# A written-out, pipelined feed-forward whose normalised rows are made on GpSimd

## Chip, cores and metric

One core of one Trainium2 chip runs the kernel. The metric is the device time of one execution in microseconds (us). TensorE does the matmuls, VectorE, ScalarE and GpSimd the rest, SyncE issues the transfers.

## What is computed

The input `x` is 8 batches of 512 rows of 256. Three blocks act on it, and two of them are followed by the same feed-forward:

```python
x = x + attn_a(layernorm(x))          # 16 heads of 16, segments of 64 rows
x = x + ffn(layernorm(x))
x = attn_b(layernorm(x))              # a recurrence over 512 steps
x = x + ffn(layernorm(x))

def _ternary_linear(x, w):            # ffn = gelu between two of these, 256 -> 1024 -> 256
    alpha = jnp.mean(jnp.abs(w))
    w_t = jnp.sign(w) * (jnp.abs(w) > 0.5 * alpha).astype(w.dtype)
    rms = jnp.sqrt(jnp.sum(x * x, axis=-1, keepdims=True)) / jnp.sqrt(d)
    return jnp.einsum('bsd,fd->bsf', x / (rms + EPS), w_t)
```

So the ternary weights need the mean of all absolute weights first, and each feed-forward output row is divided by a root of the sum of squares of its 1024 hidden values.

## The kernel before

All of `x` stays on chip as 32 tiles of 128 rows (tile `b * 4 + u` is part `u` of batch `b`). Each engine has its own instruction stream, in the order the program writes it; counted semaphores (`F[...]` for the feed-forward, `A[...]` for the attention) join the streams. There is no planner.

**Attention** works batch by batch in units `w` (16 per batch, written out). Beside it, VectorE runs a scan over the absolute weights (`scan_lanes`, L1157), four pieces of 512 per batch, for which ScalarE takes the absolute values (L784) and SyncE loads the pieces; so all 32 pieces end with the last batch. After the last batch, TensorE transposes the sums (L592), and VectorE makes the convolution taps (L1207 to L1213), the thresholds (L1216 to L1225) and both ternary weight matrices (L1230, L1232), one after the other.

**Feed-forward** (`ffn_pe`, `ffn_act`, `ffn_dve`; called with 0 and with 1) is a loop over the 8 batches. For one batch of four tiles: VectorE takes statistics (L310 to L317), ScalarE a root (L286), VectorE scales (L322 to L326) and makes the normalised rows `xn` (L330). TensorE transposes them (L223), ScalarE writes the high half (L267), VectorE the low half (L341) of `xh`, each fp16. Then eight parts `n`: up matmuls (L237), Gelu (L274), high half (L282) and square (L283) on ScalarE, low half (L344) and sum of squares (L353, L356) on VectorE, down matmuls (L248). At the end come the sums over partitions (L253), ScalarE's root of them (L288), two small VectorE instructions (L361, L363) and the four rows sums back into `x` (L368). The root is in another activation table than Gelu, so ScalarE loads a table twice per batch (L274, L286). Eleven matmuls per batch (L226, L258) compute nothing that is used. The parts have two buffers: the Gelu of part `n` waits for the low half of part `n - 2`, and TensorE's order is up `n`, down `n - 1`. The transposes of the next batch stand behind all of this one's parts. The first feed-forward also takes the statistics that the recurrence needs (L295 to L302).

**Recurrence**: 512 steps on VectorE with GpSimd, ScalarE and TensorE beside it. GpSimd has no part in the feed-forward; in attention it takes eight small roots (L1394, L1397).

## Time and profile before

| what | value |
|---|---|
| median of 3 runs | 2784.52 us (2775.18 to 2790.23) |
| the profiled execution's own time | 2776.15 us |
| its span | 2774.3 us |
| VectorE, TensorE, ScalarE, GpSimd busy | 81%, 72%, 58%, 31% |
| granted TensorE clock, mean | 0.789 of 2.4 GHz |

The profile is of one execution. Busy shares are averages over stages with different limits: the attention takes about 466 us, the first feed-forward about 200, the recurrence with what lies around it about 1880, the second feed-forward about 208.

### The profile page before, as it was taken

What the parts mean: (1) busy time and instruction counts of PE and PEld (TensorE: products, weight loads), DVE (VectorE), ACT (ScalarE), POOL (GpSimd) and SP (SyncE); (2) the same over time, 40 slices, a digit from 0 to 9 for tenths busy, and PEclk for the clock granted to TensorE, in tenths of its full rate; (3) what the DMA queues carried; (4) which work ended last, traced back from release to release, by engine and by line L of the source; (5) the groups of instructions that cost most, each with busy time, mean ns of one, the idle gap of its engine ahead of it and who ended that gap; (6) DMA issues with size and microseconds to landing.
All of it is one profiled execution on the core that took longest, in us unless ns stands there. A gap on an engine that the chain in (4) does not pass through costs nothing. (4 is left out here: it accounts for less than half of the span.)

```text
span 2774.3 us, 47870 instructions
## 1 busy us (share of the span) xinstructions
PE 2001.7 (72%) x12529; PEld 1603.4 (58%) x12529; DVE 2252.9 (81%) x5774; ACT 1617.8 (58%) x4760; POOL 855.1 (31%) x1490
## 2 busy tenths in 40 slices
PE   6888886776877777677777777777786673435777
PEld 3555554443777666677666766767676662323444
DVE  6887886777059999999999999999999999991666
ACT  4888885775455555555555555555555554443676
POOL 0000000000034544545445454444545445440000
PEclk8999997999987776777777777776676766555999
DMA  5010000000000000000000000000000000000000
GB/s 161 16 27 18 16 22 9 0 0 0 0 1 0 0 0 0 0 1 0 0 0 0 0 0 0 0 0 0 0 0 1 0 0 0 0 0 0 15 23 23
DMA packets 14188, 23.28 MB, mean 8 GB/s; under 512 B 1280, under 2 KB 12032, under 8 KB 13824
## 3 DMA queue, kind: packets, MB, share of 16 engines
q1 hardware_dynamic: 14080, 21.97, 2.7%
q8 instruction: 52, 0.85, 0.1%
q14 instruction: 56, 0.46, 0.1%
HBM read 12.27 MB, written 4.19 MB: 6 GB/s over the span
## 5 line engine op out<-in xcount | busy, mean ns | idle before, releaser
L1458 POOL TENSOR_TENSOR wu<-U,stg 128x256 f32<-128x256 f32 x512 | 318.6, 622 | 853.3 <-DVE U L1385 853.3
L621 PE MATMUL bank<-U,ident 128*128 128x128 f32 x2080 | 471.1, 398 | 122.5 <-ACT go L883 103.7
L621 PEld LDWEIGHTS bank<-U,ident 128*128 128x128 f32 x2080 | 435.1, 253 | 163.7 <-issue 74.0
L684 PE MATMUL bank<-stack,tm 128*128 128x64 f32 x1792 | 349.5, 384 | 213.2 <-ACT tm L820 213.2
L1020 ACT ACTIVATE xs<-U 128x256 f32<-128x256 f32 x512 | 213.4, 417 | 469.4 <-DVE U L1385 467.6
L684 PEld LDWEIGHTS bank<-stack,tm 128*128 128x128 f32 x1792 | 338.2, 294 | 233.6 <-issue 233.6
L1335 DVE TENSOR_REDUCE pn<-xs 128x32 f32<-128x512 f32 x512 | 351.2, 686 | 29.2
L1415 POOL TENSOR_TENSOR kv<-stg 128x256 f32<-128x256 f32 x513 | 318.8, 621 | 1.6
L607 PE MATMUL bank<-wcat,yT 128*128 x1024 | 299.5, 452 | 3.0 <-issue 3.0
L949 ACT ACTIVATE small<-pn 128x16 f32<-128x16 f32 x513 | 110.8, 216 | 305.4 <-DVE pn L1335 305.4
L607 PEld LDWEIGHTS bank<-wcat,yT 128*128 128x128 f32 x1024 | 245.9, 251 | 30.7 <-issue 18.2
L1325 DVE TENSOR_TENSOR xs<-U,bank 128x256 f32<-128x256 f32 x512 | 215.3, 421 | 31.8 <-DVE U L1385 5.5
L1339 DVE TENSOR_TENSOR bank<-pn,bank 128x256 f32<-128x256 f32 x512 | 219.4, 429 | 17.8
L1347 DVE TENSOR_TENSOR bank<-wu,bank 128x256 f32<-128x256 f32 x512 | 218.8, 427 | 15.9 <-POOL wu L1458 0.7
L1385 DVE TENSOR_TENSOR U<-bank,kv 128x256 f32<-128x256 f32 x512 | 217.0, 424 | 17.6
L742 ACT ACTIVATE prob<-bank,nmax 128x128 f32<-128x128 f32 x512 | 181.3, 374 | 39.5 <-DVE nmax L1108 38.7
L248 PE MATMUL bank<-wdn,hh 128*128 128x256 f16 x1024 | 132.4, 272 | 65.9 <-ACT hh L282 41.0
L1379 DVE TENSOR_TENSOR kv<-bank,kv 128x256 f32<-128x256 f32 x384 | 163.0, 425 | 13.8 <-DVE bank L1363 0.4
L1411 POOL TENSOR_TENSOR stg<-R 128x128 f32 (+1 forms) x65 | 29.9, 460 | 461.6 <-ACT stg L904 461.6
L344 DVE SCALAR_TENSOR_TENSOR hh<-h,hh 128x512 f16<-128x512 f32 x128 | 88.2, 689 | 92.5 <-ACT hh L282 92.3
L248 PEld LDWEIGHTS bank<-wdn,hh 128*128 128x128 f16 x1024 | 92.6, 97 | 121.9 <-ACT hh L282 56.6
L820 ACT ACTIVATE tm<-bank 64x448 f32<-64x448 f32 x256 | 137.2, 536 | 17.3 <-PE bank L607 13.4
(185 smaller groups left out, 3753.6 us busy)
## 6 DMA issues: line engine op xcount, KB each, us to landing
out_x<-x SPq DMA_DIRECT2D x8, 512.0 KB, 2.9
x<-in_x SPq DMA_DIRECT2D x1, 3584.0 KB, 16.7
Vs<-V SPq DMA_DIRECT2D x8, 384.0 KB, 4.7
Vs<-V SPq DMA_DIRECT2D x8, 288.0 KB, 3.3
lane<-in_lanes SPq DMA_DIRECT2D x8, 256.0 KB, 5.1
wcat<-in_wcat SPq DMA_DIRECT2D x1, 1792.0 KB, 13.9
wraw<-in_w_up SPq DMA_DIRECT2D x1, 1024.0 KB, 18.6
wraw<-in_w_down SPq DMA_DIRECT2D x1, 1024.0 KB, 11.4
```

The lines of the kernel that those rows point to most:

```text
L248: last = pe.matmul(bank[4 + u][:, 0:D], hh[:, e % 2, part, u * P:(u + 1) * P], wdn[:, e, :], start=(e == 0 and part == 0), stop=(e == NF - ...
L607: last = pe.matmul(bank[1 + g][:, e * PB * H:(e + 1) * PB * H], yT[:, (pc // 2) % 2, k, pc % 2, 4 * g + 2 * e:4 * g + 2 * e + 2, :].rearra ...
L621: last = pe.matmul(rsum.rearrange("p (t i) -> p t i", i=HD), ident[:, :], steps[:, :, :, j], start=(j == 0), stop=(j == HD - 1))
L684: last = pe.matmul(bank[3 + g][:, e * CH:(e + 1) * CH], tm[:, g * (PB // 2) + e, :, :].rearrange("p a c -> p (a c)"), stack[:, :], start=T ...
L1020: act.activation(xs[:, 1, :], U[:, half, j, :], ACT.Square).then_inc(S["sq"], 1)
L1325: dve.tensor_tensor(ij(xs[:, 0, :]), u, row(kkz[:, jj, 0, :]), ALU.mult).then_inc(S["x"], 1)
L1335: dve.tensor_reduce(pn[:, :, :].rearrange("p a i -> p (a i)"), xs[:, :, :].rearrange("p a (i j) -> p (a i) j", j=HD), AXX, ALU.add).then_i ...
L1339: dve.tensor_tensor(ij(zz), col(pn[:, 0, :]), row(kkz[:, jj, 1, :]), ALU.mult).then_inc(S["z"], 1)
L1347: dve.tensor_tensor(zz, wu[:, :], zz, ALU.subtract).then_inc(S["d"], 1)
L1385: dve.tensor_tensor(U[:, half, j, :], zz, new, ALU.add).then_inc(S["u"], 1)
L1415: pool.tensor_tensor(ij(kv0[:, j % 2, :]), col(stg[:, half, j, TK, :]), row(stg[:, half, j, TV, :]), ALU.mult).then_inc(S["k0"], 1)
L1458: pool.tensor_tensor(ij(wu[:, :]), ij(U[:, half if j else 1 - half, (j - 1) % STEPS, :]), col(stg[:, half, j, TW, :]), ALU.mult).then_inc( ...
```

## The change

Five things change, all in and around the feed-forward:

1. The loop over batches becomes a written-out run over 8 **groups** `q`. A group is one tile from each of four batches (`tile(q, u)`), not four tiles of one batch. The output transfers follow the groups.
2. The groups are pipelined. TensorE transposes group `q + 1` between the parts 4 and 6 of group `q`, ScalarE and VectorE split it in the parts 5 to 7 (`xh` has two copies), and the outputs of group `q - 1` are scaled and added in the parts 2 to 5 of group `q`. Two output accumulators share one bank of PSUM, so that two groups fit.
3. GpSimd takes both roots (a power of 0.5) and makes the rows `xn` of the next group. ScalarE's roots and their table loads go, and so do the eleven unused matmuls.
4. The scan gets five pieces per attention batch and is done in batch 6. Thresholds, ternary weights, taps and the rows of group 0 are made by VectorE inside the last attention batch (`last_batch`).
5. The first of the eight sums of squares is no longer copied: the second part adds both squares.

```diff
+        def tile(q, u):
+            return ((q % 2) * 4 + u) * NT + q % B // 2
+        def tiles(q):
+            return slice(tile(q, 0), tile(q, NT - 1) + 1, NT)
...
+            def rows_transposed(q, k):
+                pe.wait_ge(F["xn"], q * NT + NT)
+                if q >= 2:
+                    pe.wait_ge(F["sr"], q if q % B == 0 else q - 1)
+                    pe.wait_ge(F["lo"], (q - 1) * KD + k + 1)
+                for u in range(NT):
+                    last = pe.transpose(bank[k][:, u * P:(u + 1) * P], xn[:, u, k * P:(k + 1) * P], ident[:, :])
+                last.then_inc(F["xt"], 1)
...
+            def up(q, n):
+                t = q * NF + n
+                if n == 0:
+                    pe.wait_ge(F["hi"], q * KD + KD)
+                    pe.wait_ge(F["lo"], q * KD + KD)
+                if t >= 2:
+                    pe.wait_ge(F["g"], t - 1)
+                for part in range(2):
+                    for k in range(KD):
+                        last = pe.matmul(bank[2 + n % 2][:, :], wup[:, k, n * P:(n + 1) * P], xh[:, q % 2, part, k, :],
+                                         start=(part == 0 and k == 0), stop=(part == 1 and k == KD - 1))
+                last.then_inc(F["up"], 1)
...
+                if e == 0 and q >= 2:
+                    pe.wait_ge(F["x"], (q - 1) * NT)
...
-                pe.wait_ge(F["g"], b * NF + NF)
-                for _ in range(6):
-                    pe.matmul(bank[2][:, :], identh[:, :], wup[:, 0, 0:512], start=True, stop=True)
...
+            for k in range(KD):
+                rows_transposed(i * B, k)
+            for q in range(i * B, i * B + B):
+                for n in range(NF):
+                    up(q, n)
+                    if q > i * B or n > 0:
+                        down(q * NF + n - 1)
+                    if n == 1 and q > i * B:
+                        square_sums(q - 1)
+                    if n in (4, 5) and q < i * B + B - 1:
+                        rows_transposed(q + 1, n - 4)
+            down((i * B + B) * NF - 1)
+            square_sums(i * B + B - 1)
...
-                act.wait_ge(F["ve"], b * 2 + (2 * i + 4))
-                act.activation(sd[:, :, :], vv[:, :, :], ACT.Sqrt).then_inc(F["sd"], 1)
-                act.wait_ge(F["sm"], b + 1)
-                act.activation(ysc[:, 0, :], bank[0][:, 0:NT], ACT.Sqrt, scale=1.0 / FF).then_inc(F["sr"], 1)
...
+                    if n in (5, 6) and q < i * B + B - 1:
+                        split_high(q + 1, n - 5)
...
+            for q in range(q0, q9 + 1):
+                for n in range(NF):
+                    t = q * NF + n
+                    dve.wait_ge(F["hh"], t + 1)
+                    dve.scalar_tensor_tensor(hh[:, t % 2, 1, :], h[:, t % 2, :], HI_H, hh[:, t % 2, 0, :],
+                                             ALU.mult, ALU.subtract).then_inc(F["hl"], 1)
+                    if n >= 1:
+                        s = q * (NF - 1) + n - 1
+                        dve.wait_ge(F["sq"], t + 1)
+                        if n == 1:
+                            old = hsq[:, 1 - t % 2, :]
+                        else:
+                            old = ssq[:, (s - 1) % 3, :]
+                            dve.wait_ge(F["ss"], s)
+                        if n == 3:
+                            dve.wait_ge(F["sm"], q)
+                        dve.tensor_tensor(ssq[:, s % 3, :], old, hsq[:, t % 2, :], ALU.add).then_inc(F["ss"], 1)
+                    if q < q9:
+                        if n == 0:
+                            row_stats(dve, q + 1)
+                            row_moments(dve, q + 1)
+                        if n == 2:
+                            row_scales(dve, q + 1)
+                        if n in (6, 7):
+                            split_low(q + 1, n - 6)
+                    if q > q0:
+                        if n == 2:
+                            read_sums(q - 1)
+                        if n == 4:
+                            output_scales(q - 1)
+                        if n in (4, 5):
+                            add_rows(q - 1, (2 * n - 8, 2 * n - 7))
+                        if i == 0 and n in (6, 7):
+                            next_stats(q - 1, (2 * n - 12, 2 * n - 11))
+                        if i == 0 and n == 7:
+                            next_moments(q - 1)
...
+        def ffn_pool(pool, i, beside_first):
+            def row_roots(q):
+                pool.wait_ge(F["ve"], 2 * q + 2)
+                pool.tensor_tensor(sd[:, :, :], vv[:, :, :], halves[:, :, :], ALU.pow).then_inc(F["sd"], 1)
+            def output_roots(q):
+                pool.wait_ge(F["sr"], q + 1)
+                pool.tensor_tensor(ysc[:, 1, :], ysc[:, 0, :], halves[:, 0, :], ALU.pow).then_inc(F["s1"], 1)
+            q0, q9 = i * B, i * B + B - 1
+            def rows_normalised(q):
+                pool.wait_ge(F["sc"], q + 1)
+                pool.wait_ge(F["xt"], q * KD)
                 for u in range(NT):
...
+                    pool.tensor_scalar(xn[:, u, :], x[:, tile(q, u), :], mv[:, u, 0:1],
+                                       rstd[:, u:u + 1], ALU.subtract, ALU.mult).then_inc(F["xn"], 1)
+            row_roots(q0)
+            for q in range(q0, q9 + 1):
+                if q < q9:
+                    row_roots(q + 1)
+                    rows_normalised(q + 1)
+                if q > q0:
+                    output_roots(q - 1)
+            output_roots(q9)
...
-                    if (w - 5) % 3 == 0 and w < 17:
-                        c = (w - 5) // 3
-                        act.wait_ge(w_ld, b * 16 + 16)
-                        act.activation(lane[:, c * PIECE:(c + 1) * PIECE], lane[:, c * PIECE:(c + 1) * PIECE],
-                                       ACT.Abs).then_inc(w_abs, 1)
+                    if (w - 5) % 3 == 0 and b * PIECES + (w - 5) // 3 < 4 * B:
+                        c, piece = divmod(b * PIECES + (w - 5) // 3, 4)
+                        part = lane[:, piece * PIECE:(piece + 1) * PIECE]
+                        act.wait_ge(w_ld, c * 16 + 16)
+                        act.activation(part, part, ACT.Abs).then_inc(w_abs, 1)
...
+            def last_batch(w):
+                if w == 5:
+                    thresholds()
+                if w in (6, 7, 8, 9):
+                    ternary((w - 6) // 2, w % 2)
+                if w == 11:
+                    convolution_taps()
+                if w == 13:
+                    row_stats(dve, 0)
+                    row_moments(dve, 0)
+                if w == 15:
+                    row_scales(dve, 0)
+                    rows_normalised(dve, 0, range(NT))
...
+                    if b == B - 1 and w == 4:
+                        pe.wait_ge(w_car, B + 1)
+                        pe.wait_ge(A["rp"], B * 6 * NT)
+                        pe.transpose(bank[3][:, 0:2 * LANES], carry[:, 0:1].to_broadcast([2 * LANES, P]),
+                                     ident[0:2 * LANES, 0:2 * LANES]).then_inc(w_lan, 1)
```

How the streams move. **VectorE**, from part 7 of one batch to its outputs, before (`den`, `rstd` are the scales of the next batch, `ysc` those of the outputs):

```order
L344 SCALAR_TENSOR_TENSOR hh<-h,hh 128x512
L356 TENSOR_TENSOR ssq<-ssq,hsq 128x512
L321 REGISTER_ALU
L322 SCALAR_TENSOR_TENSOR den<-sd 128x4
L324 RECIPROCAL rstd<-den 128x4
L326 TENSOR_SCALAR rstd<-rstd 128x4
L328 REGISTER_ALU
L330 TENSOR_SCALAR xn<-x,mv,rstd 128x256 x4
L361 TENSOR_SCALAR ysc<-ysc 128x4
L363 RECIPROCAL ysc<-ysc 128x4
L368 ISA
L368 SCALAR_TENSOR_TENSOR x<-bank,ysc,x 128x256
```

VectorE now, from part 2 of a group to part 4 (L391 is the low half, L403 the sum of squares, L327 to L331 the scales of the next group, L347 the sums of the group before, L351 and L353 its output scales):

```order
L391 SCALAR_TENSOR_TENSOR hh<-h,hh 128x512
L403 TENSOR_TENSOR ssq<-ssq,hsq 128x512
L327 SCALAR_TENSOR_TENSOR den<-sd 128x4
L329 RECIPROCAL rstd<-den 128x4
L331 TENSOR_SCALAR rstd<-rstd 128x4
L347 TENSOR_SCALAR ysc<-bank 128x4
L391 SCALAR_TENSOR_TENSOR hh<-h,hh 128x512
L403 TENSOR_TENSOR ssq<-ssq,hsq 128x512
L391 SCALAR_TENSOR_TENSOR hh<-h,hh 128x512
L403 TENSOR_TENSOR ssq<-ssq,hsq 128x512
L351 TENSOR_SCALAR ysc<-ysc 128x4
L353 RECIPROCAL ysc<-ysc 128x4
```

The scales stand between parts, the four instructions for `xn` are gone from this engine, and the output scales stand two parts behind the scales.

**GpSimd**, from the attention into what follows, before:

```order
L1395 UNCONDITIONAL_BRANCH
L1395 ISA
L1397 TENSOR_TENSOR sd<-vv,halves 128x4
L1395 REGISTER_ALU
L1395 COMPARE_AND_BRANCH
L1411 TENSOR_TENSOR stg<-R 128x8x16
L1401 TENSOR_TENSOR wtmp<-wtmp,decay 128x128
```

GpSimd now, in the first feed-forward (L433 the root of the statistics, L444 the rows `xn`, L437 the root of the output sums; `ISA` is an instruction that sets the engine up):

```order
L433 TENSOR_TENSOR sd<-vv,halves 128x8 x2
L444 ISA
L444 TENSOR_SCALAR xn<-x,mv,rstd 128x256 x4
L433 TENSOR_TENSOR sd<-vv,halves 128x8
L444 TENSOR_SCALAR xn<-x,mv,rstd 128x256 x4
L437 TENSOR_TENSOR ysc<-ysc,halves 128x4
```

The four rows instructions stand ahead of the output root in GpSimd's order, and TensorE's transposes wait for all four.

**VectorE in the last attention batch**, now (L1193 maxima, L1200 a copy, L1223 and L1229, L1231 the outputs, L1266 and L1270 the ternary weights); before, none of L1266 and L1270 stood here, and a scan piece (L1157) stood in every third unit:

```order
L1193 TENSOR_REDUCE nmax<-bank 128x4
L1266 TENSOR_SCALAR wneg<-wraw,thr 128x2048
L1193 TENSOR_REDUCE nmax<-bank 128x4
L1200 COPY probT<-bank 128x512
L1270 SCALAR_TENSOR_TENSOR wup<-wraw,thr,wneg 128x2048
L1229 TENSOR_TENSOR x<-x,bank 128x256
L1231 TENSOR_TENSOR x<-x,bias_a 128x256
L1193 TENSOR_REDUCE nmax<-bank 128x4
L1214 RECIPROCAL rden<-den_a 128x16
L1216 COPY rdx<-rden 128x256
L1266 TENSOR_SCALAR wneg<-wraw,thr 128x2048
```

The long weight instructions now stand between the maxima of neighbouring units.

## Rows read from the trace of the kernel before

**Rows 1.** Busy time by stage, whole core: stretch, then busy us (instructions), PEclk, DMA.

```profile
330.00:385.00 55.00, 46.65 (x635) 29.61 (x632) 44.42 (x95) 47.60 (x181) 0.00 (x0) 1.00 0.08 19
...
424.00:466.00 42.00, 33.84 (x451) 21.78 (x449) 25.23 (x48) 28.45 (x121) 0.00 (x0) 0.83 0.01 2
...
466.00:486.00 20.00, 4.91 (x19) 2.99 (x20) 15.62 (x42) 2.80 (x5) 0.00 (x0) 0.53 0.00 0
...
2574.00:2772.00 198.00, 150.66 (x971) 90.95 (x969) 133.40 (x334) 139.78 (x237) 0.00 (x0) 1.00 0.06 19
```

**Rows 2.** Timeline from attention to the end of the first feed-forward: start us, us, engine.

```profile
465.51 0.42 DVE L1146 TENSOR_TENSOR x<-x,bias_a 128x256 f32<-128x256 f32 x1
...
478.80 0.21 ACT L262 ACTIVATE sd<-vv 128x8 f32<-128x8 f32 x1 [15.32 <-DVE vv L317]
...
479.66 1.38 DVE L330 TENSOR_SCALAR xn<-x,mv,rstd 128x256 f32<-128x256 f32 x4
...
481.10 1.97 PE L223 MATMUL bank<-ident,xn 128*128 128x128 f32 x8 [15.84 <-DVE xn L330]
...
485.89 0.60 ACT L274 ACTIVATE h<-bank 128x512 f32<-128x512 f32 x1 [0.89 <-PE bank L237]
...
683.75 0.17 DVE L302 COPY mean_b<-mv_b 128x8 f32<-128x8 f32 x1
```

**Rows 3.** Timeline of the second feed-forward, from one batch into the next.

```profile
2592.52 0.95 PE L253 MATMUL bank<-ones,ssq 128*128 128x1 f32 x8
...
2595.01 1.09 PE L223 MATMUL bank<-ident,xn 128*128 128x128 f32 x8 [0.22 <-DVE xn L330]
...
2595.78 1.09 ACT L267 ACTIVATE xh<-bank 128x512 f16<-128x512 f32 x2 [2.10 <-PE bank L223]
...
2597.00 1.28 DVE L341 TENSOR_TENSOR xh<-bank,xh 128x512 f16<-128x512 f32 x2
...
2598.52 1.90 PE L237 MATMUL bank<-xh,wup 128*128 128x512 f16 x8 [1.34 <-DVE xh L341]
...
2599.59 0.60 ACT L274 ACTIVATE h<-bank 128x512 f32<-128x512 f32 x1 [1.42 <-PE bank L237]
...
2600.22 0.63 ACT L282 ACTIVATE hh<-h 128x512 f16<-128x512 f32 x1
...
2600.88 0.69 DVE L344 SCALAR_TENSOR_TENSOR hh<-h,hh 128x512 f16<-128x512 f32 x1 [2.60 <-ACT hh L282]
...
2601.67 1.03 PE L248 MATMUL bank<-wdn,hh 128*128 128x256 f16 x8 [1.26 <-ACT hh L282]
```

**Rows 4.** Chain of waits in the same stretch: start us, us, what.

```profile
2601.67 1.03 PE bank L248 x8
...
2602.70 0.88 PE bank L237 x4
...
2605.73 1.03 PE bank L248 x8
...
2623.34 1.05 PE bank L237 x4
```

**Rows 5.** Groups of instructions by line: count, busy us, mean ns, idle before.

```profile
L324 DVE RECIPROCAL rstd<-den 128x4 f32<-128x4 f32 x18 | 3.2, 178 | 0.6
...
L1420 POOL TENSOR_SCALAR ge<-ge 128x256 f32<-128x256 f32 x64 | 54.6, 854 | 5.4
...
L1406 POOL TENSOR_SCALAR stg<-wtmp 128x128 f32<-128x128 f32 x65 | 42.0, 646 | 0.4 <-ACT wtmp L918 0.4
...
L1397 POOL TENSOR_TENSOR sd<-vv,halves 128x4 f32<-128x4 f32 x6 | 6.0, 1008 | 281.8 <-DVE vv L1063 281.8
...
L1157 DVE TENSOR_TENSOR_SCAN lane<-lane 32x512 f32<-32x512 f32 x24 | 30.4, 1265 | 0.0
```

**Rows 6.** Timeline inside the recurrence: VectorE and GpSimd at the same moment.

```profile
1500.25 0.42 DVE L1325 TENSOR_TENSOR xs<-U,bank 128x256 f32<-128x256 f32 x1
...
1500.30 0.62 POOL L1458 TENSOR_TENSOR wu<-U,stg 128x256 f32<-128x256 f32 x1 [1.14 <-DVE U L1385]
```

## Prediction before the run

> **What bounds the kernel now.** I read the windows by stage first, then the timelines of the two places that the change touches, then the chain of waits. The windows [rows 1] show what it can reach: the second feed-forward keeps TensorE busy for 151 of 198 us at a granted clock of 1.00 (the higher of its two levels, 2.4 GHz), ScalarE for 140, VectorE for 133. So no engine is full, and the stage goes by a chain. Rows 4 show that chain: two parts take 2605.73 - 2601.67 = 4.06 us, and one batch 24.82 (from the up matmuls at 2598.52 [rows 3] to those at 2623.34). The 4.06 are the loop through two buffers: the down matmuls and the up matmuls behind them 1.03 + 0.88 [rows 4], then Gelu to high half 0.63, to low half 0.66, to the next down matmuls 0.79 [rows 3], and some 0.07 of handing over between them. Eight parts so cost 16.3 us, and 8.5 of 24.8 lie between batches: table loads, roots, rows, transposes and splits, one after another [rows 3]. The other place is the way from attention to the first feed-forward [rows 2]: attention's last VectorE instruction ends at 465.93, and the first Gelu starts at 485.89. In these 20 us TensorE does 4.9 us of work at half the clock [rows 1].
>
> **One group of the new feed-forward.** It keeps the loop of the two buffers, so its floor is again 16.3 us. To it come, on TensorE or in front of it:
> - the sums of squares, 0.95, and the transposes, 1.09 [rows 3]; both now stand between parts.
> - a wait for `xn`. Count from the start of the low half of part 2. VectorE does that and the sum (0.6 each from start to start, as the two splits in rows 3 stand), then three scale instructions (0.18 [rows 5] and a little for waiting on one another): at 1.9, handing over included, GpSimd can begin. TensorE starts down 2 at 0.8 (0.69 and 0.1), up 4 at 1.7, down 3 at 2.7 (it needs the next low half) and is free for the transposes at 3.6. GpSimd's four rows instructions are not in the trace: nearest is its tensor_scalar of the same size at 0.854 us [rows 5]. Bounds are 0.62, its two-input instruction of that size [rows 6], and 1.01, its dearest [rows 5]. I take 0.85: `xn` is there at 1.9 + 3.4 + 0.1 = 5.4, TensorE waits 1.8.
> - the end of the group. The next up needs the second low half of `xh`, and VectorE makes that only behind part 7. Up 7 to its Gelu takes 1.03 and one more Copy of 0.55 ahead of it on ScalarE [rows 3], then 0.63, 0.66 to the low half, another 0.6 and 0.6 for it and the sum, 0.68 for the split, 0.1: 4.9 to 5.2, where a part takes 2.04. So 3.0 more.
> - less 0.9, since the parts beside these waits run shorter than 2.04, having been held back before.
>
> Sum 16.3 + 2.0 + 1.8 + 3.0 - 0.9 = **22.3 us**, against 24.8. The statistics of VectorE (behind part 0) and, in the first feed-forward, those for the recurrence lie beside the sums of squares and the end of the group. GpSimd's output root (1.01) stands behind `xn` and keeps VectorE waiting for about 1 us in part 4, with nothing due in that time: the low half of part 5 comes 2 us later, behind the transposes. Per 0.1 us that a rows instruction takes longer, the group takes 0.4 longer, both feed-forwards 5.6.
>
> **What GpSimd and VectorE do to each other** is the unknown. In the recurrence an instruction of VectorE with one operand in SBUF and one in PSUM takes 0.42 us beside a running one of GpSimd, and this pair stands there 512 times [rows 6]: nothing is lost. But low half and sum of squares read two tensors in SBUF, and none of that kind meets GpSimd anywhere in this trace. The lower end is nothing (22.3). The upper end is that each waits for the other's whole instruction. Then low halves and sums of parts 3 and 4 step in between the four, the root and `xn` wait for them and they for `xn`: about 3.1 us (three or four times 0.69, and 0.6 on the way back), 25.4 a group. Between: GpSimd's tensor_scalar takes 0.646 for 128 elements and 0.854 for 256 [rows 5], so 0.41 of 0.85 grows with the elements. If only this part collides, two of VectorE's instructions step in, 1.2 us: **23.5** a group. I take this, nearest to what rows 5 show of how such an instruction spends its time.
>
> The Trainium skill has a rule that speaks against the change: the page "SBUF — State Buffer", section "SBUF: two separate sides", says that a VectorE instruction with two SBUF inputs and a GpSimd instruction that reads SBUF exclude each other for the whole instruction. By it the upper end would hold. No row here can show it; it is rival B.
>
> **The sum**, against the profiled execution's own 2776.15 us:
> - Both feed-forwards, from the first group to the last: 7 x (24.82 - 23.5) = 9.2 each, -18.5. First and last group change ends that about cancel: the last roots cost 1.01 on GpSimd, a table load of 1.28 goes.
> - Way into the first feed-forward. The rows of group 0 are ready in the last attention batch, so TensorE transposes at 466.05 instead of 481.10 [rows 2]. Then as before: -14.6 after the splits. TensorE now has no unused matmuls to raise its clock: the eight transposes take 1.97 instead of 1.09 [rows 2, 3], and its first up matmuls are slow too: +1.5.
> - The last attention batch takes over what VectorE did from 465.93 to the end of the rows at 481.04 (taps, thresholds, weights, statistics, scales, rows; 15.1 us [rows 2]) and gives up four scan pieces of 1.27 [rows 5]: +10 on an engine that is idle for 17 of the last 42 us [rows 1], which is 1 us per unit, in the gaps between units. Between 0 and 10; half hidden, +5.
> - Six more scan pieces in batches 0 to 5, where VectorE is idle for 10.6 of 55 us [rows 1], and two fewer in batch 6: 4 x 1.27 = 5, half hidden: +2.5. SyncE's order of piece and shifted values keeps both a unit or two ahead: 0.
> - Into the second feed-forward: GpSimd's root 1.01 for ScalarE's 0.21 [rows 5, 2], +0.8, and the colder clock, +1.
> - Output transfers are as large as before and the last is again one: 0. Written-out code: 0.
>
> Sum -18.5 - 14.6 + 1.5 + 5 + 2.5 + 1.8 = **-22 us**, 2754 for such an execution. Its time lies 8 us below the median of the runs shown, so against 2784.5 I forecast **2762 us**.
>
> **Rivals.**
> - A, no collision: 22.3 a group, 7 x 1.2 x 2 = 17 less, 2745. For it: rows 6. Against: they have no instruction with two SBUF operands. 0.25.
> - B, whole instructions exclude each other: 25.4, 27 more than forecast, 2789. The feed-forward then loses 8 us, and only the way into it gains. 0.25.
> - C, slower: as B, and a rows instruction with its two per-partition scalars takes more than the tensor_scalar of rows 5, which has none. From 1.03 us on the kernel is over 0.5% slower (0.18 x 56 = 10 on top of B's 4); at 1.2 it takes 2808. Place: the transposes in part 4, which wait for all four. 0.12.
> - D, slower: the clock. The unused matmuls are gone; where the granted clock falls to its lower level, the blocks of matmuls of 0.88 us [rows 4] take twice as long. If that holds for a quarter of the 16 in a group, it is 3.5 us a group, 49 in all: 2811. Against: TensorE is busy for 16 of 23.5 us, not far from the 151 of 198 at 1.00 [rows 1], and waits longer than 2 us only at the transposes. 0.05.
> - Forecast: 0.33 and within 10 us of 2762 for the attention's half-hidden terms.
>
> **Numbers.** 0.5% is 14 us, about what a measurement here can tell from none. Faster by more holds A and three quarters of the forecast: 0.50. Within it are B and the rest of the forecast: 0.31. Slower: C, D and the edge of B, 0.19. The range runs from A with a gain in the last batch, 2738, to B with 10 us more, 2799.
>
> **What would show it.** In the profile after: distance of first up matmuls between groups 23.5 (22.3 in A, 25.4 in B); GpSimd's `xn` instructions at 0.85 and idle time of VectorE or stretched low halves beside them; idle time of TensorE before the transposes of part 4, released by GpSimd, 3 us; first Gelu near 480; last attention batch 5 us longer; granted clock 1.00 in both feed-forwards. A clock below 0.9 there, or first Gelu later than 486, would make the prediction wrong.

## The result, and the profile after

The change makes the kernel slower: 2822.3 us median of 4 runs (2803.7 to 2827.0) against 2783.4 (2775.2 to 2790.2) before, ratio 1.013 with a 95% interval of 1.007 to 1.018. Forecast were 2762 us and a range from 2738 to 2799. The profiled execution took 2826.6 us (span 2824.5), 50 more than that of before. By stage, between the same events of the two traces:

| stretch | before | after | difference |
|---|---|---|---|
| start to the end of attention's last add | 465.9 | 484.6 | +18.7 |
| from there to the first Gelu | 20.0 | 5.4 | -14.6 |
| first Gelu to the last add of feed-forward 1 | 195.9 | 220.9 | +25.0 |
| recurrence with both ways, to the next first Gelu | 1893.0 | 1896.4 | +3.4 |
| feed-forward 2 | 196.0 | 213.8 | +17.8 |

So the way into the first feed-forward paid what was forecast, and both feed-forwards, which should have become 9 us shorter each, became longer. The first Gelu starts at 490.1, 4 us later than before, because attention ends later; a start behind 486 was one of the prediction's signs of being wrong, and so was a clock below 0.9. The windows by stage show the clock (columns as in [rows 1]):

```profile
484.00:712.00 228.00, 161.02 (x896) 97.41 (x896) 135.06 (x366) 119.92 (x209) 66.75 (x43) 0.83 0.00 1
2622.00:2822.00 200.00, 141.18 (x833) 86.47 (x831) 110.76 (x265) 108.83 (x191) 61.40 (x38) 0.88 0.06 19
```

The granted clock, 1.00 in the second feed-forward before [rows 1], is 0.88 there and 0.83 in the first. The timeline of the way into the first feed-forward, which answers to [rows 2]:

```profile
484.20 0.42 DVE L1231 TENSOR_TENSOR x<-x,bias_a 128x256 f32<-128x256 f32 x1
...
484.73 1.94 PE L230 MATMUL bank<-ident,xn 128*128 128x128 f32 x8 [1.02 <-issue]
...
490.07 0.60 ACT L299 ACTIVATE h<-bank 128x512 f32<-128x512 f32 x1 [1.47 <-PE bank L242]
```

The transposes begin 0.1 us behind the last add, at the lower clock level (1.94 us for eight). The timeline of the second feed-forward, parts 3 and 4 of a group, answers to [rows 3] (start us, us, engine):

```profile
2642.76 6.88 POOL L444 TENSOR_SCALAR xn<-x,mv,rstd 128x256 f32<-128x256 f32 x4 [2.23 <-DVE rstd L331]
2642.77 0.71 DVE L391 SCALAR_TENSOR_TENSOR hh<-h,hh 128x512 f16<-128x512 f32 x1
2643.40 0.68 DVE L403 TENSOR_TENSOR ssq<-ssq,hsq 128x512 f32<-128x512 f32 x1
...
2643.62 1.03 PE L254 MATMUL bank<-wdn,hh 128*128 128x256 f16 x8
...
2644.93 0.69 DVE L391 SCALAR_TENSOR_TENSOR hh<-h,hh 128x512 f16<-128x512 f32 x1 [0.86 <-ACT hh L304]
...
2649.61 1.02 POOL L437 TENSOR_TENSOR ysc<-ysc,halves 128x4 f32<-128x4 f32 x1
...
2649.69 1.08 PE L230 MATMUL bank<-ident,xn 128*128 128x128 f32 x4 [5.04 <-POOL xn L444]
...
2650.57 1.91 PE L242 MATMUL bank<-xh,wup 128*128 128x512 f16 x4
2650.67 0.17 DVE L351 TENSOR_SCALAR ysc<-ysc 128x4 f32<-128x4 f32 x1 [4.44 <-POOL ysc L437]
...
2652.52 0.60 ACT L299 ACTIVATE h<-bank 128x512 f32<-128x512 f32 x1 [7.10 <-PE bank L242]
```

This is the place. GpSimd begins `xn` at 2642.76, 0.1 us behind the scales, and takes **6.88 us for four instructions**, where I had 3.4 without a collision and 4.6 with the one that I took. VectorE's low halves and sums go on beside it at 0.68 to 0.71. TensorE waits 5.04 us, ScalarE's next Gelu 7.10, and VectorE 4.44 for the output root, which stands behind `xn`. TensorE then works on at 1.91 instead of 1.03.

Eleven of the fourteen groups look like this. In the other three TensorE waits only 3.4 to 3.5 us, and in two of them VectorE is held up too. One of the two, in the first feed-forward:

```profile
583.45 5.70 POOL L444 TENSOR_SCALAR xn<-x,mv,rstd 128x256 f32<-128x256 f32 x4 [3.74 <-DVE rstd L331]
...
583.69 0.85 DVE L391 SCALAR_TENSOR_TENSOR hh<-h,hh 128x512 f16<-128x512 f32 x1
```

There the low half starts 0.24 us behind the first rows instruction and not 0.01. It takes 0.85 instead of 0.69, and the four rows instructions take 5.70 instead of 6.88.

The chain of waits of the second feed-forward (answers to [rows 4]) has it twice:

```profile
2642.76 6.89 POOL xn L444 x4
...
2649.69 1.08 PE bank L230 x4
2650.78 1.71 PE bank L242 x4
...
2658.26 2.27 issue
2660.53 1.86 PE bank L242 x4
```

Behind the wait a block of four up matmuls takes 1.71 where [rows 4] had 0.88. The same happens behind the 2.27 us between groups (2660.53). First up matmuls of neighbouring groups are 28.0 us apart here (2632.56 to 2660.53) and 27.4 from group to group on the average of this feed-forward, against 24.8. The groups by line (answers to [rows 5]: busy us, mean ns, idle before):

```profile
L444 POOL TENSOR_SCALAR xn<-x,mv,rstd 128x256 f32<-128x256 f32 x56 | 92.8, 1667 | 31.1 <-DVE rstd L331 31.1
...
L391 DVE SCALAR_TENSOR_TENSOR hh<-h,hh 128x512 f16<-128x512 f32 x128 | 88.9, 695 | 126.8 <-ACT hh L304 126.5
...
L433 POOL TENSOR_TENSOR sd<-vv,halves 128x8 f32<-128x8 f32 x16 | 30.4, 1900 | 427.3 <-DVE vv L323 427.3
```

VectorE's low halves have a mean of 695 ns, against 689 before, the two held up included. GpSimd's rows instruction has a mean of 1667 ns, and in the eleven groups the four take 2.25, 2.24, 1.22 and 1.22.

### The profile page after: what moved, and what is told of

Read it like the earlier page. It is cut to its first block and busy times, and to the rows that moved or that the text cites. A ratio compares the mean times of both kernels' runs of the same rounds, so it can differ in the third digit from the quotient of the medians.

```text
span 2824.5 us, 46550 instructions
## 1 busy us (share of the span) xinstructions
PE 2024.0 (72%) x12353; PEld 1613.5 (57%) x12353; DVE 2224.8 (79%) x5672; ACT 1568.7 (56%) x4695; POOL 992.4 (35%) x1578
## 5 line engine op out<-in xcount | busy, mean ns | idle before, releaser
L1445 DVE TENSOR_TENSOR bank<-pn,bank 128x256 f32<-128x256 f32 x512 | 219.5, 429 | 17.8
L391 DVE SCALAR_TENSOR_TENSOR hh<-h,hh 128x512 f16<-128x512 f32 x128 | 88.9, 695 | 126.8 <-ACT hh L304 126.5
L242 PE MATMUL bank<-xh,wup 128*128 128x512 f16 x512 | 158.5, 441 | 36.6 <-issue 33.7
L433 POOL TENSOR_TENSOR sd<-vv,halves 128x8 f32<-128x8 f32 x16 | 30.4, 1900 | 427.3 <-DVE vv L323 427.3
L299 ACT ACTIVATE h<-bank 128x512 f32<-128x512 f32 x128 | 76.3, 596 | 186.1 <-PE bank L242 185.4
L254 PE MATMUL bank<-wdn,hh 128*128 128x256 f16 x1024 | 147.3, 291 | 20.5 <-DVE hh L391 18.5
```

The lines of the kernel that those rows point to most:

```text
L1445: dve.tensor_tensor(ij(zz), col(pn[:, 0, :]), row(kkz[:, jj, 1, :]), ALU.mult).then_inc(S["z"], 1)
```

## The experiments

My theory after this reading: three things add up. The rows instruction takes 1.22 us by itself; VectorE holds it up; and TensorE's long wait costs a second time by the clock.

The kernels below were measured in three further rounds, each together with the kernel before, whose median was 2774.9, 2775.9 and 2780.7 us there and 2783.4 in the round of the change. So two medians from different rounds can be out against one another by some 8 us. Differences from the change are given by medians; by the ratios to the kernel before they are smaller for what gained: 64 us instead of 81 for e1, 21 instead of 32 for e3, 23 instead of 36 for e4.

### e1: the rows back on VectorE

```diff
                         if n == 2:
                             row_scales(dve, q + 1)
+                        if n == 2:
+                            rows_normalised(dve, q + 1, range(NT))
...
                     row_roots(q + 1)
-                    rows_normalised(q + 1)
```

> Edit: the four rows instructions go back to VectorE, behind the scales in part 2; GpSimd keeps both roots. Theory (GpSimd's rows instruction, 1.22 us alone and 2.24 beside a low half and a sum, makes TensorE wait 5.04 us per group, and the clock falls behind that wait): the wait before the transposes is gone (under 0.5 us), the granted clock in both feed-forwards is back at 0.95 or more, a group takes about 22 us instead of 27.7, so 14 x 5.7 = 80 us less than the change: about 2742, faster than the kernel before. Rival 1 (the clock falls because the eleven unused matmuls are gone, whatever the wait): clock stays near 0.85, group near 24, about 2770. Rival 2 (GpSimd's roots or the order of the outputs hold the group): group stays over 26, no less than 2800.

2741.5 us, ratio to before 0.990 (0.986 to 0.994), as expected. Which engine makes the rows decides, by itself, between slower and faster. The timeline of its second feed-forward:

```profile
2632.19 1.38 DVE L337 TENSOR_SCALAR xn<-x,mv,rstd 128x256 f32<-128x256 f32 x4
...
2633.72 3.19 POOL L439 TENSOR_TENSOR ysc<-ysc,halves 128x4 f32<-128x4 f32 x1 [3.39 <-DVE ysc L347]
...
2634.39 1.03 PE L254 MATMUL bank<-wdn,hh 128*128 128x256 f16 x8 [1.28 <-DVE hh L391]
...
2635.26 0.60 PE L230 MATMUL bank<-ident,xn 128*128 128x128 f32 x4
...
2644.37 1.02 PE L242 MATMUL bank<-xh,wup 128*128 128x512 f16 x4 [2.28 <-issue]
```

Four rows take VectorE 1.38 us, TensorE transposes without any wait, and this group takes 21.2 us (2623.19 to 2644.37); the average is 21.6 in the second and 22.5 in the first feed-forward. The granted clock is 0.96 in its second and 0.93 in its first feed-forward, with no unused matmul: rival 1 is out as the main cause, though the clock, which was 1.00 before, is still down behind the wait of 2.28 us between groups in some of them. The output root on GpSimd, 1.02 in the change, now takes 3.19 beside four of VectorE's long instructions; VectorE waits 0.90 for it.

### e3: VectorE's work beside the rows made small

```diff
+                    e = slice(0, 1 if n in (3, 4) else L)
-                    dve.scalar_tensor_tensor(hh[:, t % 2, 1, :], h[:, t % 2, :], HI_H, hh[:, t % 2, 0, :],
+                    dve.scalar_tensor_tensor(hh[:, t % 2, 1, e], h[:, t % 2, e], HI_H, hh[:, t % 2, 0, e],
...
-                        dve.tensor_tensor(ssq[:, s % 3, :], old, hsq[:, t % 2, :], ALU.add).then_inc(F["ss"], 1)
+                        dve.tensor_tensor(ssq[:, s % 3, e], old[:, e], hsq[:, t % 2, e], ALU.add).then_inc(F["ss"], 1)
```

> Edit: low half and sum of squares of parts 3 and 4, the two parts beside which GpSimd makes the rows, work on one element instead of 512; that part of the computation is left out, all else stays. Theory (VectorE's instructions with two SBUF operands hold GpSimd up by 1.03 us per pair): all rows instructions take 1.22, four of them 4.9 instead of 6.88, none takes 2.2; TensorE waits 3.0 instead of 5.04; group 2 us or more shorter, at least 28 us less than the change, about 2790. Rival (the 2.2 us are GpSimd's own, the first instructions of such a run are long): four still take 6.9, wait of TensorE stays over 4.5, kernel within 8 us of the change.

2790.0 us (ratio 1.005, 1.003 to 1.008). The instructions of the tile `xn` (min/median/max ns, and who waited):

```profile
L445 POOL TENSOR_SCALAR xn<-x,mv,rstd x56: 1217/1219/1229, 493.6 to 2748.0; 128x256 f32<-128x256 f32 x56
...
  PE bank L230: 44.1, 14
```

All 56 take 1.22 us, so the 2.25 is VectorE's doing, and the 1.22 is GpSimd's own. TensorE waits 3.15 on the average (44.1 / 14). Both feed-forwards together, counted as in the table of stages, take 402 us instead of 435: the collision costs the change some 32 us, its share of the clock included, and so say the medians; by the ratios it is 21.

Behind one and the same wait the clock does two things in this run. Transposes and the up matmuls behind them, in two groups of the first feed-forward:

```profile
548.62 0.66 PE L230 MATMUL bank<-ident,xn 128*128 128x128 f32 x4 [3.16 <-POOL xn L445]
549.11 1.03 PE L242 MATMUL bank<-xh,wup 128*128 128x512 f16 x4
...
601.63 1.12 PE L230 MATMUL bank<-ident,xn 128*128 128x128 f32 x4 [3.16 <-POOL xn L445]
602.54 1.91 PE L242 MATMUL bank<-xh,wup 128*128 128x512 f16 x4
```

The group of the first pair takes 24.3 us at a granted clock of 0.93, that of the second 27.3 at 0.82. Of the seven distances between groups, four are 27.3 in the first feed-forward and one is in the second, and most of the others 24.0 to 24.5.

### e10: only the sum of squares made small

The second line of e3's edit alone.

> Edit: the change, with the sum of squares alone of parts 3 and 4 on one element (that part of the computation is left out); the low halves beside GpSimd's rows instructions stay whole. With both, an instruction of GpSimd took 2.24 instead of 1.22; with neither 1.22 (e3). Theory (each instruction of VectorE with two SBUF operands holds GpSimd up by half of 1.03): the longest rows instruction takes 1.7 to 1.75, four take 5.9, TensorE waits 4.0. Rival 1 (the sum alone, both of whose inputs and output are four-byte, does it): all near 1.25. Rival 2 (the low half alone does it): longest still 2.2, four 6.9.

2812.1 us (ratio 1.012), by the medians 10 less than the change and by the ratios 3. Neither rival: the longest is 1.73, so one low half costs 0.52. But four took 5.34, not the 5.9 of the theory, and TensorE waits 3.50, not 4.0. The tile's instructions, then the timeline of one group:

```profile
L445 POOL TENSOR_SCALAR xn<-x,mv,rstd x56: 1213/1217/1733, 490.7 to 2769.8; 128x256 f32<-128x256 f32 x56
```

```profile
2656.40 4.14 POOL L445 TENSOR_SCALAR xn<-x,mv,rstd 128x256 f32<-128x256 f32 x3 [2.98 <-DVE rstd L331]
2656.41 0.71 DVE L391 SCALAR_TENSOR_TENSOR hh<-h,hh 128x512 f16<-128x512 f32 x1
...
2658.57 0.69 DVE L391 SCALAR_TENSOR_TENSOR hh<-h,hh 128x512 f16<-128x512 f32 x1 [1.39 <-ACT hh L304]
```

The first rows instruction begins within 0.01 us of a low half and takes 1.732. The second begins at 2658.11 and takes 1.216, though a low half runs inside it from 2658.57, itself at its usual 0.69. So a GpSimd instruction is held up at its beginning; one that was 0.46 us under way was not, and did not hold VectorE up either.

The shorter wait brings little time, because the clock takes it back: groups of the second feed-forward still take 27.3 us, at a granted clock of 0.83 where the change had 0.88.

### e7: constants instead of per-partition scalars

```diff
-                    pool.tensor_scalar(xn[:, u, :], x[:, tile(q, u), :], mv[:, u, 0:1],
-                                       rstd[:, u:u + 1], ALU.subtract, ALU.mult).then_inc(F["xn"], 1)
+                    pool.tensor_scalar(xn[:, u, :], x[:, tile(q, u), :], 0.25,
+                                       2.0, ALU.subtract, ALU.mult).then_inc(F["xn"], 1)
```

> Edit: the change, with GpSimd's rows instruction taking two constants instead of the two per-partition scalars (mean and scale), so that groups 1 to 7 are not normalised. Measures what was mis-sized: the one-operation tensor_scalar with a constant took 0.854 in the kernel before, the rows instruction 1.22 alone. Theory (the per-partition scalars cost the difference): 0.85 to 0.9 alone, four with two VectorE pairs beside them 5.5 instead of 6.88, TensorE waits 3.7 instead of 5.04, and about 20 us less than the change, near 2800. Rival (the second operation costs it, not the scalars): still 1.22 alone, kernel within 6 us of the change.

2793.9 us (ratio 1.007). Neither side:

```profile
L444 POOL TENSOR_SCALAR xn<-x x56: 1062/1112/1432, 499.6 to 2754.6; 128x256 f32<-128x256 f32 x56
...
  PE bank L230: 38.4, 14
```

With constants it takes 1.06 alone, so the two scalars per partition cost 0.16. The remaining 0.21 up to the 0.854 of [rows 5] lie between one operation and two, but also between different operations (that one is a minimum). Four take 4.85 where I had 5.5, because the collision has changed as well:

```profile
2630.78 4.85 POOL L444 TENSOR_SCALAR xn<-x 128x256 f32<-128x256 f32 x4 [2.20 <-DVE rstd L331]
2630.80 0.92 DVE L391 SCALAR_TENSOR_TENSOR hh<-h,hh 128x512 f16<-128x512 f32 x1
```

The low half that starts 0.02 us behind the first of them takes 0.92 instead of 0.69, and that rows instruction keeps its 1.07; the next two take 1.43 and 1.37. So only 0.6 of the collision (4.85 - 4 x 1.06) is left on GpSimd's side, and e7 does not price the scalars alone. TensorE waits 2.74 (38.4 / 14), and the kernel is 28 us faster than the change by the medians, 17 by the ratios, where I had 20.

### e4: unused matmuls in TensorE's waits

```diff
+                    if n == 4 and q < i * B + B - 1:
+                        for _ in range(18):
+                            pe.matmul(bank[3][:, :], identh[:, :], wup[:, 0, 0:512], start=True, stop=True)
                     if n in (4, 5) and q < i * B + B - 1:
                         rows_transposed(q + 1, n - 4)
+                    if n == NF - 1 and q < i * B + B - 1:
+                        for _ in range(8):
+                            pe.matmul(bank[2][:, :], identh[:, :], wup[:, 0, 0:512], start=True, stop=True)
```

> Edit: unused matmuls are put back, 18 ahead of the transposes in part 4 (3.8 us at the higher level, inside TensorE's wait of 5.04) and 8 ahead of a group's first up matmuls. Rows stay on GpSimd. Theory (the wait costs a second time by the clock): granted clock of both feed-forwards 0.97 or more, blocks of four up matmuls 0.88 instead of 1.71 behind the transposes, wait for the rows itself unchanged at its end, group 27.7 to 25.8, 27 us less than the change, about 2795. Rival (the clock follows something else than TensorE's waits, as the two levels over the whole run): clock stays below 0.9 and the kernel is 0 to 30 us slower, the unused matmuls being paid at the lower level.

2786.2 us (ratio 1.0045, 1.002 to 1.007), 36 us less than the change, by matmuls that compute nothing. Timeline and window of its second feed-forward:

```profile
2671.88 4.05 PE L281 MATMUL bank<-wup,identh 128*128 128x512 f16 x18
2677.09 0.66 PE L230 MATMUL bank<-ident,xn 128*128 128x128 f32 x4 [1.16 <-POOL xn L450]
2677.58 1.03 PE L242 MATMUL bank<-xh,wup 128*128 128x512 f16 x4
2678.45 1.04 PE L254 MATMUL bank<-wdn,hh 128*128 128x256 f16 x8
```

```profile
2622.00:2785.00 163.00, 141.70 (x879) 83.10 (x877) 98.04 (x234) 93.82 (x166) 57.16 (x37) 1.00 0.07 23
```

The rows come as late as before, but the blocks behind them take 0.87 from start to start (2677.58 to 2678.45), the clock is 1.00, and a group takes 25.2 us in each of the last six. In the same six the change takes 27.5 on the average, so 2.3 of them are the clock. The other 25.2 are still more than the 24.8 of the kernel before: the rows on GpSimd cost more than the pipelining gained even at the full clock.

### e2, e5, e6: the fourth item undone

```diff
-PIECES = 5
+PIECES = 4
...
-                    if b == B - 1:
-                        last_batch(w)
...
             dve.wait_ge(A["x2"], B * NT)
+            for w in range(5, 16):
+                last_batch(w)
```

with the transpose of the sums behind the last batch again. e2 is this on the change, e5 on e1, and e6 is e5 with five scan pieces per batch.

> Edit: change without its fourth item: four scan pieces per attention batch again, and thresholds, weights, taps and rows of group 0 behind the last attention batch. Theory (what the last batch took over cost 18.7 us there and saved 14.6 on the way, a loss of 4 net): last residual add back near 466, first Gelu near 486 to 488, kernel 2815 to 2825, the same as the change within 5 us. Rival (attention's later end has another cause, such as the place of the code or the recurrence's buffers): last add still after 478, and the kernel 10 us or more slower than the change.

> Edit: rows on VectorE as in e1, and the fourth item undone as in e2 (four scan pieces per batch, thresholds, weights, taps and rows of group 0 behind the last attention batch). Against e1 it prices the fourth item. Theory (in single profiles, last add at 457.1 and way to the first Gelu 19.5 us in e2, 477.9 and 2.7 in e1): the two end within 5 us of each other, 2737 to 2747, last add some 20 us earlier than in e1, way 17 us longer. Rival (the item gains what it took off the way): 2752 or more. Rival (it costs net, as the profiles alone say, 4 us and more): under 2736.

> Edit: as e5, but with five scan pieces per attention batch, done in batch 6. So only the scans have moved, and the last batch has neither scans nor anything else beside it. Theory (a piece of 1.27 us is about half hidden in batches 0 to 6): about 3 us on e5 from the pieces, less what the empty last batch gives back (4 pieces, up to 5 us): within 3 us of e5. Rival (VectorE's pieces cost in full in batches 0 to 6): 5 us or more slower than e5. What the last batch itself costs when it takes over 15 us of work is then e1's last add less this one's.

e2 2831.2 us (ratio 1.021, 1.018 to 1.025); e5 2744.0 (0.989, 0.986 to 0.992); e6 2748.1 (0.989). e1, e5 and e6 cannot be told from one another: beside rows on VectorE the item that I had down for -14.6 + 5 + 2.5 = -7 is worth nothing to 5 us. Beside rows on GpSimd it looks worth more: I expected e2 within 5 us of the change, and it is 9 slower by the medians and 24 by the ratios. Why, these runs don't show. Nor was e5's last add 20 us earlier than e1's, as I expected: it was at 477.0 against 477.9. Where the item's gain goes can be read from single profiles, with care: the ten profiles with the new last batch (the change, e1, e3, e4, e7 to e12) have the end of attention's last add between 468.8 and 488.1, median 485, the three with the old end and four pieces (e2, before, e5) at 457.1, 465.9 and 477.0, e6 at 472.2, and the way that is saved is 17 us each time (22.3 in e2 and e5 against 5.4). One execution differs from the next by 19 us in the same attention code, so no single pair of them gives this price.

### e11: transposes one part later, rows on GpSimd

```diff
-                    if n in (4, 5) and q < i * B + B - 1:
-                        rows_transposed(q + 1, n - 4)
+                    if n in (5, 6) and q < i * B + B - 1:
+                        rows_transposed(q + 1, n - 5)
```

and the same for ScalarE's high halves.

> Edit: the change, with the transposes of the next group and their high halves one part later (parts 5 and 6, high halves in 6 and 7); rows stay on GpSimd. Theory (GpSimd's rows are merely late where they are asked for): TensorE waits 5.04 less a part of 2.1, so 2.9; the clock stays up behind a wait of that size as in e3 and e7; group 27.6 to between 23 and 24, kernel 2755 to 2775, faster than the change by 50 us and the same as before or a little better, but no better than rows on VectorE (e1, 2741). Rival (the end of the group is held up by what was gained, since high and low half of the second transposes are now behind part 7): group over 25, kernel over 2785.

2800.6 us (ratio 1.008): the wait is as expected, the time is not. The profiled execution took 2785.5, the fastest of five.

```profile
2668.36 0.66 PE L230 MATMUL bank<-ident,xn 128*128 128x128 f32 x4 [2.89 <-POOL xn L444]
2668.85 1.57 PE L242 MATMUL bank<-xh,wup 128*128 128x512 f16 x4
2671.37 1.86 PE L254 MATMUL bank<-wdn,hh 128*128 128x256 f16 x8 [0.95 <-DVE hh L391]
...
2679.12 1.59 PE L242 MATMUL bank<-xh,wup 128*128 128x512 f16 x4 [2.28 <-issue]
```

TensorE waits 2.89 for the rows, but also 0.95 for the next low half and 2.28 between groups, and blocks of 1.86 (clock 0.90) stand behind them. Groups take 23.5 to 28 us, 26.0 on the average of the second feed-forward. The numbers of the rival have come (group over 25, kernel over 2785), but its cause shows little: the wait between groups of the second feed-forward is 2.28 to 2.45 us, where the change had 2.28. My expectation took the clock from e3 as if it had held behind every wait of 3.16, which it had not. The rescue of GpSimd's rows by a later use is worth 22 us by the medians and 14 by the ratios, against the 81 and 64 of e1.

### e8, e9, e12: towards a version that beats both

e8 is e1 with the second low half of the next group's rows ahead of part 7's low half; e9 makes two of the rows in part 3; e12 gives the fourth row of e9 to GpSimd.

```diff
+                    if n == 7 and q < q9:
+                        split_low(q + 1, 1)
                     dve.wait_ge(F["hh"], t + 1)
...
+                    if n == 3 and q < q9:
+                        rows_normalised(dve, q + 1, (2, 3))
```

> Edit: e1 with the second low half of the next group's rows ahead of the low half of part 7 instead of behind its sum. In e1 a group takes 21.2 us, and TensorE waits 2.28 of them before the next group's first up matmuls. Theory (that wait is the last thing between groups): first up matmuls start 1.4 us earlier, group 19.8, 14 x 1.4 = 20 us less than e1, about 2720. Rival (the low half of part 7 comes later and the time is lost at the down matmuls of part 7, or at the clock): within 6 us of e1.

> Edit: e8, with VectorE's four rows instructions in two places: two behind the scales in part 2, two between the low half and the sum of part 3. In e8 the four take 1.38 us at once and the low half of part 3 comes late (TensorE waits 1.28 for it). Theory: that wait shrinks by 0.7 and TensorE's transposes still find their rows, group 19.6 to 18.9, about 10 us less than e8: near 2703. Rival (the rows are now late for the transposes, or another wait takes the place): within 4 us of e8's 2712.6.

> Edit: e9, with the fourth rows instruction on GpSimd and three on VectorE. Asks whether GpSimd can take any of this work. Theory (one instruction takes 1.22 alone and 2.24 beside VectorE's, and TensorE asks for it 1.7 us behind the scales): it is late by 0.6 us or about as much as VectorE gains, same as e9 within 4 us. Rival 1: it frees VectorE by 0.35 us per group and is hidden, 5 us faster than e9. Rival 2: it holds the transposes up in full, 8 us or more slower than e9.

e8 2712.6 us (ratio 0.977, 0.973 to 0.980). The timeline of TensorE in its second feed-forward:

```profile
2619.54 1.03 PE L254 MATMUL bank<-wdn,hh 128*128 128x256 f16 x8 [1.28 <-DVE hh L393]
2620.41 0.60 PE L230 MATMUL bank<-ident,xn 128*128 128x128 f32 x4
...
2627.97 1.02 PE L242 MATMUL bank<-xh,wup 128*128 128x512 f16 x4 [0.72 <-issue]
...
2640.03 0.60 PE L230 MATMUL bank<-ident,xn 128*128 128x128 f32 x4
```

The wait between groups is 0.72 instead of 2.28 and a group 19.6 (2620.41 to 2640.03). That is 29 us less than e1, where I expected 20. e9: 2708.0 (0.974, 0.972 to 0.976), a group 19.0; the gain on e8 is 5 us in the medians where 14 x 0.6 = 8 were to be had by the groups. **e9 beats both kernels**, and its windows show why more than order was won:

```profile
484.00:650.00 166.00, 136.62 (x898) 85.73 (x896) 140.11 (x390) 119.22 (x209) 24.38 (x15) 0.97 0.00 1
2560.00:2700.00 140.00, 121.16 (x817) 76.86 (x815) 114.52 (x283) 106.91 (x190) 21.95 (x14) 1.00 0.08 27
```

Clock 0.97 and 1.00, without one unused matmul. e12: 2710.4 (0.974, 0.971 to 0.976), the same. GpSimd can take one row, for which it needs 1.36 us there; it gains nothing.

## Why the prediction was wrong

- **Which part went where.** In the profiles the change came out at +50 us where the sum had -22, 73 off. Both feed-forwards are 61 of it (+42.8 for -18.5), attention is 11 (+18.7 for +7.5). The way into the first feed-forward came out at -14.6 where the sum had -14.6 + 1.5: the kernel before had the slow transposes too (1.97 [rows 2]), so most of the +1.5 was no difference. The group (24.8 to 23.5) came out at 27.4 in the second feed-forward and 28.1 in the first. This is the step that failed: what GpSimd's rows cost TensorE in wait and in clock.
- **The size of the rows instruction** is the first term that was mis-sized. I took 0.85 from a tensor_scalar with one operation and a constant, and bounded it by 1.01, the dearest instruction on GpSimd. It takes 1.22 (e3). A bound taken from other forms of instruction was no bound: by my own 0.4 per 0.1 us it gives +1.5 us a group. This case stood as rival C with 0.12.
- **The collision** was forecast as 1.2 us, with rival B's 3.1 above it. It was 2.0 (6.88 - 4 x 1.22) in eleven of the fourteen groups, all of it on GpSimd's side, and less in three, where the low half began 0.16 to 0.55 us behind. 23.5 + 1.5 + 0.8 = 25.8; e4, where the clock is held up, shows 25.2. So the terms of the group were sound but for these two. (They add up to 22.2 and not to the 22.3 that I wrote; that is 1.4 us in all.)
- **The clock** (rival D, 0.05) is the other 2.3. I had it as a case by itself, against which spoke that TensorE waits longer than 2 us only at the transposes. But my own sum had 3.0 for the end of the group, and there TensorE waits 2.27. And the wait at the transposes was the one that C makes longer: C and D are one case, and their prices add. C alone would have given 2808, the kernel took 2822. What the clock costs is no fixed sum: with the same waits e3 has groups of 24.0 and of 27.3 us.
- **Rival B's rule.** The Trainium skill ("SBUF — State Buffer", "SBUF: two separate sides") has whichever starts first hold the other off entirely. In e10 the later one, 0.46 us behind, was not held off, and it ran inside the other at its usual 0.69. Each engine does hold the other up near the beginning of the rows instruction: GpSimd loses 1.03 us to a low half and a sum that start with it, VectorE's low half takes 0.85 when it starts 0.24 behind. So the rule holds here for a part of the instruction and not for its whole length.
- **The last batch.** +10 on VectorE, "half hidden", and +2.5 for the scan pieces stand against about +19 by the medians of the profiles' last adds. These spread over 19 us among kernels with the same attention code, so the size is rough, and the medians of e1, e5 and e6 only say that item four nets nothing to 5 us where I had -7. I counted VectorE's free time and not that a weight instruction of 2.34 us stands between the maxima of neighbouring units, which TensorE and ScalarE wait for. That this is the reason is argued from the order of the instructions; no run took it alone.
- **GpSimd's order.** The output root behind `xn` kept VectorE waiting 4.44 us where I had about 1, "with nothing due" as forecast: the low half of part 5 came behind the transposes anyway.

## What to carry to other kernels

Work given to an engine that is idle is priced by the form of the instruction on that engine, alone and beside the neighbours that it gets, and by who waits for the last of it: VectorE did in 1.38 us what took GpSimd 6.88. A wait that grew on TensorE was paid twice here, once as itself and once as the clock behind it, so a rival of a long wait and one of a fallen clock belong in one case. And before work is moved off a busy engine, try its order there: moving one VectorE instruction ahead of another brought 29 us (e8), where the rows on GpSimd had cost 64 to 81.

## What the runs showed that I had not expected

- GpSimd's two-operation tensor_scalar over 128x256 takes 1.22 us with two per-partition scalars and 1.06 with two constants; VectorE's takes 0.41 with the scalars.
- A low half of VectorE (two operands in SBUF) that starts within 0.01 us of GpSimd's rows instruction adds 0.52 us to it, low half and sum 1.03, and keeps its own 0.71. A low half that starts 0.16 or 0.24 us behind takes 0.93 or 0.85, and the rows instruction keeps its 1.22. One that starts 0.46 us behind holds nothing up and is not held up (e10). So an estimate from these is that about the first 0.4 us of the rows instruction shut the low half out (0.24 + 0.85 - 0.69), and with constants 0.25 (0.02 + 0.92 - 0.69, e7). Who is first in that stretch decides, and 0.15 us of start turned it round. The full rule is not settled by these runs.
- VectorE's own rows instruction (one tensor and two scalars per partition) is held up too: the one that starts 0.26 us behind GpSimd's takes 0.57 instead of 0.41 (e12).
- A root of four elements on GpSimd takes 1.02 us alone and 3.19 beside four instructions of VectorE (e1); one of eight takes 1.64 to 2.10 and never less.
- Whether the clock holds behind a wait of about 3 us differs from group to group in one execution: in e3 and e7 groups of 24 us, where it held, stand beside groups of 27.3, where it fell, behind the same 3.16 and 2.78 us.
